# A group of four tiles between two stretches of linears, in place of pairs, in a one-core mix and quantized linear kernel

## The reference

```
y   = einsum('bct,bcd->bdt', x, weights[condition])
w   = (unpacked 6-bit q - zero_point) * scale        # 1024 x 1024
out = x + einsum('bsk,nk->bsn', y, w) + bias
```

## Time and profile before

| | us |
|---|---|
| three runs | 292.17, 293.94, 291.20 |
| their median | 292.17 |
| the profiled execution | 291.73 |
| its span, first to last instruction | 289.9 |
| PE busy | 284.0 |
| DVE busy | 189.0 |
| POOL busy | 92.0 |
| ACT busy | 84.5 |

### The profile page before, as it was taken

The page is one execution under the profiler, slowest core; times in us unless marked ns, Lnnn a source line. Parts: engine busy times, 40 slices in busy tenths (PEclk is TensorE's granted clock), DMA queues, the critical chain, the costliest instruction groups (busy, mean ns, idle before and its releaser), DMA issues.

```text
span 289.9 us, 8492 instructions
## 1 busy us (share of the span) xinstructions
PE 284.0 (98%) x3299; PEld 233.0 (80%) x3299; DVE 189.0 (65%) x255; ACT 84.5 (29%) x195; POOL 92.0 (32%) x39
## 2 busy tenths in 40 slices
PE   7999999999999999999999999999999999999995
PEld 3777878888888888888888888888888888888884
DVE  3687998656657565665756566575656657575554
ACT  3755434502306060230606033060603306030000
POOL 1019924324043432404343240434324043430000
PEclk9999999999999999999999999999999999999999
DMA  7982666442524344152524425143442511122112
GB/s 253 308 330 81 189 215 203 146 157 75 190 75 140 123 147 152 72 161 101 174 89 145 154 77 185 72 150 112 147 152 78 184 72 42 67 75 73 74 72 73
DMA packets 20547, 39.02 MB, mean 135 GB/s; under 512 B 6835, under 2 KB 7091, under 8 KB 20532
## 3 DMA queue, kind: packets, MB, share of 16 engines
q1 hardware_dynamic: 20100, 37.63, 37.9%
q10 hardware_dynamic: 432, 1.18, 1.1%
HBM read 22.02 MB, written 16.78 MB: 134 GB/s over the span
## 4 chain that ended last, share of the span: by engine, by line
PE 93%; DMA 2%; SPq 2%; ACT 1%; DVE 1%; issue 1%
PE o_ps L301 80%; PE y_ps L259 10%; DMA q_raw<-in_L_ffn_qweight_dram 2%; PE ysum_ps L319 1%; SPq L153 1%; SPq L149 1%; ACT qT L462 1%; PE y_ps L301 1%; DMA ids<-in_itok_B_dram 0%; PE ysum_ps L273 0%; PE qt_ps L283 0%; PE ysum_ps L348 0%; ACT junk L427 0%; SPq L138 0%; DVE q_int L522 0%
## 5 line engine op out<-in xcount | busy, mean ns | idle before, releaser
L301 PE MATMUL o_ps<-qT,y_hi 128*128 128x512 f32 (+1 forms) x520 | 200.6, 389 | 0.4 <-ACT qT L462 0.4
L301 PE MATMUL o_ps<-qT,y_lo 128*128 128x512 f32 (+1 forms) x520 | 198.1, 384 | 0.0
L656 POOL TENSOR_TENSOR resid<-x_sb,bias_bc 128x1024 f32<-128x1024 f32 x32 | 90.8, 2841 | 166.1 <-DVE o_sb L560 147.2
L301 PEld LDWEIGHTS o_ps<-qT,y_hi 128*128 128x128 f32 x520 | 97.2, 188 | 21.1 <-issue 0.8
L301 PEld LDWEIGHTS o_ps<-qT,y_lo 128*128 128x128 f32 x520 | 97.2, 188 | 18.8
L552 DVE TENSOR_TENSOR o_sb<-o_ps,scale_bc 128x512 f32<-128x512 f32 x63 | 43.5, 691 | 81.0 <-PE o_ps L301 81.0
L436 ACT ACTIVATE y_hi<-y_ps 128x512 fp32r<-128x512 f32 x64 | 33.4, 603 | 159.7 <-PE y_ps L259 159.5
L560 DVE TENSOR_TENSOR o_sb<-o_sb,resid 128x512 f32<-128x512 f32 x63 | 52.7, 838 | 2.2
L532 DVE TENSOR_TENSOR y_lo<-y_ps,y_hi 128x512 fp32r<-128x512 f32 x64 | 40.0, 683 | 7.3 <-ACT y_hi L436 7.3
L541 DVE SCALAR_TENSOR_TENSOR resid<-zs_bc,ysum,resid 128x1024 f32<-128x1024 f32 x32 | 43.9, 1371 | 0.1
L259 PE MATMUL y_ps<-w_sb,x_sb 64*64 64x64 f32 x2048 | 33.9, 219 | 0.0
(11 more groups left out here) (33 smaller groups left out, 46.9 us busy)
## 6 DMA issues: line engine op xcount, KB each, us to landing
x_sb<-in_x_dram SPq DMA_DIRECT2D x32, 512.0 KB, 3.5
out_dram<-o_sb SPq DMA_DIRECT2D x63, 256.0 KB, 2.0
q_raw<-in_L_ffn_qweight_dram SPq DMA_DIRECT2D x5, 384.0 KB, 5.9
q_raw<-in_L_ffn_qweight_dram ACTq DMA_DIRECT2D x3, 384.0 KB, 5.2
w_sb<-in_L_cond_weights_dram SPq DMA_DIRECT2D x64, 16.0 KB, 2.0
bias_bc<-in_L_ffn_bias_dram SPq DMA_DIRECT2D x1, 512.0 KB, 7.9
zs_bc<-n_weight_zero_point_dram SPq DMA_DIRECT2D x1, 512.0 KB, 8.7
out_dram<-o_sb SPq DMA_DIRECT2D x2, 128.0 KB, 2.0
```

What stands on the lines that cost most here:

```text
L301: last = nc.tensor.matmul(bank, part[:, slot, kt, :], qT[:, kt, col:col + width], start=(kt == 0 and part is y_hi), stop=(kt == KT - 1 and ...
L656: nc.gpsimd.tensor_tensor(resid[:, j % RING, :], x_sb[:, j % RING, :], bias_bc[:], ALU.add).then_inc(xbias_ready, 1)
```

## The change

PE's steady part goes by trips of four tiles: row sums of four tiles, their four mixes, then their eight linear halves (`mixes`, `linears`, `last_linear`). Since four tiles' y are alive at once, y has three places of two banks in PSUM, and the fourth tile's y takes the first bank of place 0 and the right half's bank o_ps[1]. The row sums go to o_ps[0] and the second bank of place 2, in which the third tile's y follows. ysum_ps and qt_ps are gone. From this come new waits inside the group of mixes, each followed by an increment of a semaphore that nothing waits for (`third_begun`, `fourth_begun`); the right half of the group's first tile waits for all eight y_lo writes. ACT copies the sums two columns at once (`copy_sums`), in four instructions a trip rather than eight.

In the prologue the scales are no longer spread by PE: two loads copy them to each partition. Tiles 2 and 3 are mixed together, the four row sums follow in one place, and tiles 4 and 5 are mixed in the first trip of the loop. DVE scales tile 0's left half in two pieces. ACT issues q blocks 0 to 3, half of tile 0's weights and the left scales; SP issues the rest, with the tiles' x ahead of scales, zero points and bias. w_sb holds 64 columns and needs no zeroing.

```diff
-        w_sb = sb("w_sb", [P, RING, P], F32)
+        w_sb = sb("w_sb", [P, RING, S], F32)
...
-        y_ps = psum("y_ps", [P, 2, 2, KT, S], F32)
+        y_ps = psum("y_ps", [P, 3, 2, KT, S], F32)
         o_ps = psum("o_ps", [P, H, NH], F32)
-        ysum_ps = psum("ysum_ps", [P, 512], F32)
-        qt_ps = psum("qt_ps", [P, KT, P], BF16)
-
-        ysum_banks = [ysum_ps[:, :], qt_ps[:, :, :].bitcast(F32).rearrange("p t n -> p (t n)")]
-        qt_banks = [qt_ps[:, :, :], o_ps[:, 1, :].bitcast(BF16).rearrange("p (t n) -> p t n", t=KT)]
-
...
+        def y_bank(slot, half):
+            return y_ps[:, slot, half, :, :].rearrange("p t r -> p (t r)")
+
+        def as_bits(bank):
+            return bank.bitcast(BF16).rearrange("p (t n) -> p t n", t=KT)
+
+        o_banks = [o_ps[:, h, :] for h in range(H)]
+        free_banks = [y_bank(2, half) for half in range(2)]
+        y_banks = [[y_bank(slot, half) for half in range(2)] for slot in range(3)]
+        y_banks.append([y_bank(0, 0), o_banks[1]])
+        y_banks = [[bank.rearrange("p (t r) -> p t r", t=KT) for bank in pair] for pair in y_banks]
+        sum_banks = [o_banks[0], free_banks[1]]
+        qt_banks = [as_bits(free_banks[0]), as_bits(o_banks[1])]
...
+        third_begun = sem("third_begun")
+        fourth_begun = sem("fourth_begun")
...
+        def load_row(eng, dst, src, s):
+            eng.dma_start(dst, src.partition_broadcast(P)).then_inc(s, 16)
+
+        scale_line = scale.rearrange("n a -> (n a)")
+
+        def load_scale(eng, h):
+            cols = slice(h * NH, (h + 1) * NH)
+            load_row(eng, scale_bc[:, cols], scale_line[cols], scale_loaded[h])
+
+        def load_w_half(eng, slot, half, entry):
+            rows = slice(half * S, (half + 1) * S)
+            eng.dma_start(w_sb[rows, slot, :],
+                          weights[bass.ds(entry, 1), :, :].rearrange("a c s -> (a c) s")
+                          ).then_inc(w_loaded[slot], 16)
...
             load_x(0, 0)
-            sp.dma_start(scale_row[:], scale.rearrange("n a -> a n")).then_inc(scale_loaded, 16)
             sp.wait_ge(ids_loaded, 16)
-            sp.wait_ge(w_zeroed, 1)
-            load_w(0, 0)
-            load_q(sp, 3)
+            load_w_half(sp, 0, 0, pick(sp, 0))
             load_x(1, 0)
             load_w(1, 0)
             for n in range(4, NT):
                 load_q(sp, n)
-            sp.dma_start(bias_bc[:], bias.partition_broadcast(P)).then_inc(bias_loaded, 16)
-            sp.dma_start(zs_bc[:], zero.rearrange("n a -> (n a)").partition_broadcast(P)).then_inc(zero_loaded, 16)
-            load_x(2, 0)
-            load_w(2, 0)
-            load_x(3, 0)
-            load_w(3, 0)
+            for j in range(2, RING):
+                load_x(j, 0)
+                load_w(j, 0)
+            load_scale(sp, 1)
+            load_row(sp, zs_bc[:], zero.rearrange("n a -> (n a)"), zero_loaded)
+            load_row(sp, bias_bc[:], bias, bias_loaded)
 
 
             reload(4, 0)
             reload(5, 0)
             store(0, 0, 0)
+            store(0, 0, 1)
             reload(6, 0)
-            store(0, 0, 1)
-            store(1, 0, 0)
             reload(7, 0)
-            store(2, 0, 0)
-            store(1, 0, 1)
-            reload(8, 0)
-            store(2, 0, 1)
-            reload(9, 0)
-
-            def step(pair, i, loads=True):
-                if loads:
-                    for j in pair:
-                        reload(j + LOADLEAD, i)
-                for j in pair:
+            for j in range(1, RING):
+                for h in range(H):
+                    store(j, 0, h)
...
+            with sp.Fori(1, TRIPS - 1) as i:
+                for j in range(RING):
+                    reload(j + RING, i)
+                for j in range(RING):
                     for h in range(H):
                         store(j, i, h)
...
+                            last = nc.tensor.matmul(banks[half][part * Q:(part + 1) * Q, kt, :],
+                                                    x_sb[rows, slot, k0:k0 + Q], w_sb[rows, slot, :],
...
-            def wait_pair(pair, i):
-
-                for j in pair:
-                    wait_mix(j + LEAD, i)
-                    pe.wait_ge(xsum_ready, i * RING + j + LEAD + 1)
-                pe.wait_ge(ysum_ready, i * RING + pair[0] + LEAD)
...
+            def sum_y(j, banks):
 
                 slot = j % RING
                 for half in range(2):
                     rows = slice(half * C, (half + 1) * C)
-                    place = slice((half + j) % 2 * S, ((half + j) % 2 + 1) * S)
-                    last = nc.tensor.matmul(ysum_banks[half][place, slot:slot + 1], w_sb[rows, slot, rows],
-                                            xsum[rows, slot:slot + 1], start=True, stop=True)
-                    last.then_inc(ysum_ps_ready, 1)
-
-            def step(pair, i, mixes=True, ahead=True):
-                if mixes:
-                    for j in pair:
-                        sum_y_halves(j + LEAD)
-                    for j in pair:
-                        mix(j + LEAD, i)
-                a, b = pair
-                for h in range(H):
-                    linear(a, i, h)
-                linear(b, i, 0)
-                pe.wait_ge(scaled[1], i * RING + b)
-                products(o_ps[:, 1, :], NH, NH, b % RING, range(KT - 1))
-                if ahead:
-                    wait_pair((a + LEAD, b + LEAD), i)
-                products(o_ps[:, 1, :], NH, NH, b % RING, range(KT - 1, KT)).then_inc(o_ps_ready[1], 1)
+                    place = (half + j) % 2
+                    nc.tensor.matmul(banks[half][place * S:(place + 1) * S, slot:slot + 1], w_sb[rows, slot, :],
+                                     xsum[rows, slot:slot + 1], start=True, stop=True).then_inc(ysum_ps_ready, 1)
+
+            def mixes(i):
+
+                for j in range(RING):
+                    sum_y(j, sum_banks)
+                for j in range(2):
+                    mix(j, y_banks[j])
+                pe.wait_ge(ysum_ready[1], i + 1)
+                pe.sem_inc(third_begun, 1)
+                mix(2, y_banks[2])
+                pe.wait_ge(scaled[1], i * RING)
+                pe.wait_ge(y_lo_ready, i * RING * 2 + 1)
+                pe.sem_inc(fourth_begun, 1)
+                mix(3, y_banks[3])
+
+            def linears(i):
+                for j in range(RING - 1):
+                    for h in range(H):
+                        if j == 0 and h == 0:
+                            pe.wait_ge(ysum_ready[0], i + 1)
+                        if j == 0 and h == 1:
+                            pe.wait_ge(y_lo_ready, (i + 1) * RING * 2)
+                        linear(j, i, h)
+                linear(RING - 1, i, 0)
+                pe.wait_ge(scaled[1], i * RING + RING - 1)
+
+            def last_linear(i):
+
+                for kt in range(KT):
+                    if kt >= KT - RING:
+                        slot = kt - (KT - RING)
+                        pe.wait_ge(w_loaded[slot], (i + 2) * 32)
+                        pe.wait_ge(xsum_ready, (i + 1) * RING + slot + 1)
+                    if kt == KT - 1:
+                        pe.wait_ge(scaled[0], (i + 1) * RING)
+                    last = products(o_banks[1], NH, NH, RING - 1, range(kt, kt + 1))
+                last.then_inc(o_ps_ready[1], 1)
...
+            for j in (2, 3):
+                wait_mix(j, 0)
+                mix(j, y_banks[j - 2])
+            pe.wait_ge(qt_ready, 7)
+            pe.wait_ge(xsum_ready, RING)
+            for j in range(RING):
+                sum_y(j, free_banks)
             pe.wait_ge(qt_ready, NT)
             linear(0, 0, 1)
-            sum_y(2, 0)
+            for half in range(2):
+            products(free_banks[0], NH, NH, 1).then_inc(o_ps_ready[1], 1)
+            pe.wait_ge(scaled[1], 1)
+            products(o_banks[1], NH, NH, 2).then_inc(o_ps_ready[1], 1)
...
+            last_linear(0)
             with pe.Fori(1, TRIPS - 1) as i:
-                for pair in PAIRS:
-                    step(pair, i)
-            step(PAIRS[0], TRIPS - 1, ahead=False)
-            for h in range(H):
-                linear(RING - 2, TRIPS - 1, h)
-            linear(RING - 1, TRIPS - 1, 0)
-            pe.wait_ge(scaled[1], TILES - 1)
+                mixes(i)
+                linears(i)
+                last_linear(i)
+            mixes(TRIPS - 1)
+            linears(TRIPS - 1)
...
+            act.wait_ge(warm_ready, 1)
+            nc.scalar.activation(junk[:, 1, 0:1], warm[:, 0:1], ACT.Copy)
+            act.wait_ge(ids_loaded, 16)
+            load_w_half(act, 0, 1, pick(act, 1))
+            for n in range(2, NT // 2):
+                load_q(act, n)
+            load_scale(act, 0)
```

More of the change, by code:

```diff
@@ L121, in adaln_ffn @@
         ysum_ps_ready = sem("ysum_ps_ready")
-        ysum_ready = sem("ysum_ready")
+        ysum_ready = [sem(f"ysum_ready{half}") for half in range(2)]
         xbias_ready = sem("xbias_ready")
```

(53 more changed lines are left out.)

211 lines of the change are left out of this document (66 added, 145 removed).

## The result

| | before | after |
|---|---|---|
| median of 13 runs, us | 292.17 | 295.56 |
| the profiled execution, us | 291.73 | 295.56 |
| its span, us | 289.9 | 293.7 |

The account below looks back on a forecast made before the run. PE was taken as the bound, busy in 284.0 of 289.9 us. Prologue - 0.5 and loop + 0.3 made - 0.2 us, forecast 291.7 us against 292.17; own range 289.5 to 293.5, 8 in 10 287.5 to 294.8.

Parts of the forecast that it names:

- the serial sum: Prologue: POOL's additions and DVE's operations in turn from the bias's landing at 23.0 us, scaling tile 2's left half at 44.4.
- The first two rivals: Bias as early as before, 287.2 us, chance 0.24; waits among the mixes empty the array, 296.9 us, chance 0.08.
- PE waits 44.4 - 39.7 = 4.7 us for its left-half bank, and the loop begins at 44.4 + 2 x 3.68 = 51.8 us: Prologue, tile 3's left half: a 4.7 us bank wait leaves 0.5 of 5.2 us gained; loop begins at 51.8, not 52.30.
- From the loop's beginning to the last matmul this makes 234.1 - 2.1 + 2.05 + 0.35 = 234.4 us: Steady part: fewer shape changes save 2.1 us, tiles 4 and 5's mixes add 2.05, new waits 0.35; no gain.
- a bubble between the mixes: Loop's mixes: two new waits, data ready in time, sequencer cost 0.05 us a trip, 0.35 in all; bounds nothing to 0.3 a trip.
- The step from 291.5 to the forecast's median: Whole kernel: profiled execution forecast at 291.5 us, old median 0.44 above its profiled one, so 291.7 us forecast.
- the same three terms: Prologue gain of 5.2 us, wait of 4.7 us for the left-half bank after the bias, and the loop's 0.3 us loss.
- The slow side of the forecast: Whole kernel: slower by over 1%, chance 0.16.
- the emptied array: Loop's mixes: PE's increments hold the next mix until earlier ones are through, 14 x 0.4 us; 296.9 us, chance 0.08.
- late loads: Prologue: bias or q blocks land much later, 26 us or more, costing 3 us or more; 295 us, chance 0.08.
- the likeliest case: The forecast's own case: bias lands at 23.0 us, PE waits 4.7 us near 40 us; 291.7 us, chance 0.60.

Follow-up runs that it names:

- experiment 3: Changed kernel with 80 small matmuls on zeros put ahead of tile 3's left half, moving the code behind: 295.20 us, ratio 1.011 to the kernel before.
- Experiment 2: Changed kernel with 16 matmuls of 128x512 on zeros filling PE's wait ahead of tile 3's left half: 293.32 us, ratio 1.004 to the kernel before.
- Experiment 7: Changed kernel with bias and zero points loaded early, its last trip run by the loop's own code: 289.83 us, ratio 0.995 to the kernel before.
- Experiment 8: Changed prologue with early bias, and the old steady part mixing the next pair ahead of this pair's halves: 289.00 us, ratio 0.991 to the kernel before.
- experiment 1: Changed kernel with bias and zero points loaded ahead of x and weights of tiles 2 and 3: 291.13 us, ratio 0.996 to the kernel before.
- experiment 6: Changed kernel with early bias, every trip by pairs, each mixed right before its own halves: 306.07 us, ratio 1.052 to the kernel before.

## Why the prediction was wrong

**Right, point by point.** The right half of tile 0 starts at 25.04 us (25.0 forecast). That is luck in part: the gap of 0.41 us at 23.72 us stands ahead of it, and with the same code and no gap there, in experiment 3, it starts at 24.59. The bias lands at 23.1 (23.0). PE waits for line 527 at tile 3's left half until 43.77 us (44.4), and POOL's additions and DVE's operations take turns, as the serial sum had it. A middle trip takes 33.47 us (33.4 to 33.5). The third mix follows the second without a pause, the fourth after 0.07 us more than the usual step (0.05 a trip). The first two rivals did not come: the bias was not early, and the array was not emptied by PE's increments.

**The step that failed first: "PE waits 44.4 - 39.7 = 4.7 us for its left-half bank, and the loop begins at 44.4 + 2 x 3.68 = 51.8 us".** The wait was priced at its length alone. It also left the next twelve matmuls half the clock (0.50); the loop began at 53.67. That is 1.9 us above the forecast: 2.5 for the clock, less 0.6 for a wait that ended sooner. Experiment 2 gives 2.2 of it back with the wait in place. The profile of before could not show this price, since its clock is full throughout, but its 3.68 us a half was a price at full clock, and was carried behind a wait of nearly 4 us, where the wait shown late in the old prologue is 0.41.

**The step that failed next: "From the loop's beginning to the last matmul this makes 234.1 - 2.1 + 2.05 + 0.35 = 234.4 us".** It took 290.46 - 53.67 = 236.8. Two gaps of 0.92 and 1.05 us (0.93 and 1.06 less the usual step) are most of the 2.4; no run takes the other 0.4 apart. The sum costed each mix and each change of shape by the old trace, in which a pair's 256 instructions of mixes stand between linears and no gap is seen. A group of four has 512, and where they were new, PE stopped among them or right behind them in every kernel that has the group: in the loop's first trip in six of six, in a last trip with its own code in four of four. The text did look for a bubble between the mixes, but asked of the sequencer only what its steps cost. Experiment 7 shows the cause by taking the newness away, the table under 3 by where the gaps lie. Experiment 8 puts the worth of the groups in the balance: they save 33.75 - 33.47 = 0.28 us a trip, 2.0 us over seven, and the two gaps alone took 2.0 us in the changed kernel and 3.4 in experiment 1.

Together 1.9 + 2.4 = 4.3 us, less 0.25 at the end (5.10 us from the last matmul to the end of the execution instead of 5.35), are the 4.06 us between 291.5 and 295.56. (The step from 291.5 to the forecast's median is a slip: with the 0.44 that it names it gives 291.9, not 291.7. It changes nothing here.)

**The rivals** left out both: each was a version of the same three terms. The slow side of the forecast rested on the emptied array, with 0.08, and on late loads; that a wait of nearly 4 us has a price behind it deserved a rival, as it lay in the likeliest case.

**Open.** How long a gap is was not settled: 0.4 to 1.9 us, and none at all in the prologue of three kernels. The packet's own length doesn't decide it: the gap of 1.81 us in experiment 1 stands behind a packet of 1.7 us, that of 1.85 us in experiment 3 behind one of 0.93. That other transfers at that time delay the packets was not tried. Nor was it shown why the clock fell behind a gap of 1.81 us in experiment 1 and did not behind one of 1.85 in experiment 3, or why it fell in 2 of the 29 runs of the kernel before beside experiment 1 (mean granted clock 0.994; 294.1 and 294.3 us against a median of 292.0).

## What to carry to other kernels

A wait on the critical engine costs its length and can cost slow clock behind it: 2.5 us after the wait of 3.9 us here, nothing after the 14 stops of 1.3 to 1.5 us in experiment 6. Where a change creates such a wait, look for work to put into it, or better for the load that ends it (here the place of two loads among the first ones was worth 4.4 us). A long run of very short matmuls is cheap in a loop and can be dear where its code runs for the first time (at each gap of the groups of four 0.9 to 1.9 us from start to start here, and none in a loop's later trips); keep such runs short between longer work, and let the loop's own code run the last trip rather than a copy of it. The first trip is new in any case. A group that saves a fixed amount each trip should be charged with what it loses once.

## What the runs showed of the hardware

- Changed kernel: idle for 3.9 us, then 12 matmuls of 128x512 at 0.43 us instead of 0.23, at a granted clock of 0.50. With the wait filled (experiment 2), the clock stayed at 1.00. With 14 stops of 1.3 to 1.5 us (experiment 6) it stayed at 1.00 too.
- Packets of 16 KB (ten, 0.16 MB in the changed kernel) came where PE's code was new; at a gap PE went on 1.1 to 1.5 us after a packet's end. In the loop of about 820 instructions none is seen after its first trip: 5 trips without one in the changed kernel.
- With POOL at work on 128x1024, DVE's operations of 1.2 and 1.3 us on two SBUF inputs took 3.5 and 3.3 us (changed kernel, 27.88 and 31.39 us), and those of 0.7 us up to 2.7 (37.80 us). The y_lo of the kernel before, which has one input in PSUM, kept its time: two took 1.28 us at 27.36 us, with POOL at work, and 1.27 at 37.58, with POOL idle.
- Kernel before, DMA in windows of 2 us from 2 to 20 us: 228 to 405 GB/s, with a share of 0.82 at 6 to 8 us and 0.81 at 12 to 14; in the last one, 405 GB/s, the 512 KB of zero points were under way (issued at 11.0 us, landed 8.7 us later).
